# Rotary embedding of the queries moved into the score product, in the two chosen-token layers of a fused transformer kernel

## What is computed

```python
scores = h @ w_router                       # one score for each of the 1024 tokens
idx = sort(top_k(scores, 128))              # 128 tokens are chosen
x = hidden[idx]; pos = idx
h = rms_norm(x, ln1_w)
q = (h @ wq + bq)                           # 16 heads of 128
k = (h @ wk + bk); v = (h @ wv + bv)        # 8 heads of 128
q = q * cos + rotate_half(q) * sin          # rotary embedding by the token's place
k = k * cos + rotate_half(k) * sin
att = softmax(mask(q @ k.T / sqrt(128)))    # 128 x 128 for each of the 16 heads
x1 = x + (att @ v) @ wo
mlp = silu(rms_norm(x1) @ w_gate) * (rms_norm(x1) @ w_up) @ w_down
out[idx] = gate * (x1 + mlp) + (1 - gate) * x
```

## Time and profile before

| | |
|---|---|
| median of 3 runs | 1484.77 us (1483.41 to 1485.47) |
| profiled execution | 1484.15 us, of which the profile's span covers 1482.9 us |
| TensorE busy | 1408.4 us (95%) |
| VectorE busy | 1074.2 us (72%) |
| ScalarE busy | 1044.8 us (70%) |
| GpSimd busy | 686.9 us (46%) |
| mean granted TensorE clock | 0.982 of full speed |

### The profile page before, as it was taken

One profiled execution on the slowest core, in us unless ns is written; L12 is line 12 of the kernel. 1 busy time (PEld: TensorE's weight loads), 2 busy tenths in 40 slices (PEclk: granted clock), 3 DMA queues, 4 the chain that ended last, 5 costly groups with the idle time before them and its releaser, 6 DMA issues.

```text
span 1482.9 us, 23456 instructions
## 1 busy us (share of the span) xinstructions
PE 1408.4 (95%) x8326; PEld 1207.0 (81%) x8326; DVE 1074.2 (72%) x2453; ACT 1044.8 (70%) x2284; POOL 686.9 (46%) x830
## 2 busy tenths in 40 slices
PE   7899999999999998998999999999999978979899
PEld 6789898888888886787888888888897876657677
DVE  6989898989898985667766757766666737567634
ACT  4898989999898987575655655655654755585754
POOL 6576777676776646142333333433321130823223
PEclk9999999999999999999999999999999998998999
DMA  2000000000000000610000000000003332000000
GB/s 75 2 19 1 19 9 12 1 19 19 1 8 2 15 1 1 270 37 22 16 21 8 30 22 8 26 25 15 1 8 140 132 119 82 0 1 1 0 0 29
DMA packets 14340, 45.12 MB, mean 30 GB/s; under 512 B 3216, under 2 KB 3216, under 8 KB 12048
## 3 DMA queue, kind: packets, MB, share of 16 engines
q1 hardware_dynamic: 14224, 43.61, 8.2%
HBM read 42.55 MB, written 1.05 MB: 29 GB/s over the span
## 4 chain that ended last, share of the span: by engine, by line
PE 73%; DVE 16%; ACT 7%; issue 2%; POOL 1%; DVEq 0%; ACTq 0%; POOLq 0%
PE ps L149 32%; PE ps L355 16%; PE ps L344 10%; PE ps L1189 6%; DVE a_pT_lo L411 3%; DVE a_prob L364 2%; PE ps L2057 2%; PE ps L2063 2%; DVE a_q L694 1%; PE ps L2073 1%; PE ps L2076 1%; PE ps L614 1%; PE ps L2059 1%; PE ps L1964 1%; DVE h L2326 1%
## 5 line engine op out<-in xcount | busy, mean ns | idle before, releaser
L386 POOL TENSOR_SCALAR a_prob<-a_prob,a_rowinv 128x128 f32<-128x128 f32 (+7 forms) x256 | 188.4, 751 | 132.6 <-DVE a_rowinv L380 132.4
L411 DVE TENSOR_TENSOR a_pT_lo<-ps,a_pT_hi 128x512 fp32r<-128x512 f32 (+3 forms) x384 | 194.7, 550 | 21.0 <-ACT a_pT_hi L403 19.3
L364 DVE CUSTOM_DVE_ANT_0 a_prob<-ps,a_mask 128x128 f32<-128x128 f32 (+7 forms) x256 | 187.0, 749 | 21.1 <-PE ps L149 20.9
L371 ACT ACTIVATE a_prob<-a_prob,a_negmax 128x128 f32<-128x128 f32 (+7 forms) x256 | 197.3, 778 | 2.2 <-DVE a_negmax L364 1.5
L386 POOL TENSOR_SCALAR b_prob<-b_prob,b_rowinv 128x128 f32<-128x128 f32 (+7 forms) x128 | 94.4, 749 | 199.5 <-DVE b_rowinv L380 199.4
L403 ACT ACTIVATE a_pT_hi<-ps 128x512 fp32r<-128x512 f32 (+3 forms) x384 | 167.3, 492 | 24.7 <-PE ps L344 15.5
L344 PE MATMUL ps<-ident,a_prob 128*128 128x128 f32 x1152 | 160.2, 275 | 7.0 <-DVE a_pT_lo L411 5.5
L371 ACT ACTIVATE b_prob<-b_prob,b_negmax 128x128 f32<-128x128 f32 (+7 forms) x128 | 99.6, 779 | 72.5 <-DVE b_negmax L364 71.7
L344 PEld LDWEIGHTS ps<-ident,a_prob 128*128 128x128 f32 x1152 | 130.0, 140 | 20.5 <-POOL a_prob L386 7.9
L149 PE MATMUL ps<-a_k_hi,a_q 128*128 128x512 f32 (+3 forms) x384 | 140.3, 373 | 1.8 <-DVE a_negmax L364 1.2
L355 PE MATMUL ps<-a_pT_hi,a_v 128*128 128x512 f32 (+3 forms) x384 | 131.2, 349 | 1.1 <-DVE a_pT_lo L411 0.6
(11 more groups left out here) (479 smaller groups left out, 4005.7 us busy)
## 6 DMA issues: line engine op xcount, KB each, us to landing
f_wq<-in_f_wq SPq DMA_DIRECT2D x2, 2048.0 KB, 8.9
f_wo<-in_f_wo SPq DMA_DIRECT2D x2, 2048.0 KB, 18.0
b_w_raw<-in_b_qk SPq DMA_DIRECT2D x16, 256.0 KB, 2.6
a_w_raw<-in_a_w SPq DMA_DIRECT2D x8, 384.0 KB, 3.2
a_vo<-in_a_o SPq DMA_DIRECT2D x8, 256.0 KB, 2.6
f_wk<-in_f_wk SPq DMA_DIRECT2D x2, 1024.0 KB, 11.0
f_wv<-in_f_wv SPq DMA_DIRECT2D x2, 1024.0 KB, 13.0
f_wg<-in_f_wg SPq DMA_DIRECT2D x2, 1024.0 KB, 19.9
```

Source lines behind the costliest of these rows:

```text
L364: dve.tensor_tensor_reduce(slot(a, u), g.ps_flat[:, bank * HALF:bank * HALF + width], a.mask[:, N - width:], -1.0, -MASKED, ALU.add, ALU.m ...
L371: act.activation(prob, prob, ACT.Exp, bias=a.negmax[:, n:n + 1], scale=-1.0, accum_out=a.rowsum[:, n:n + 1]).then_inc(*g.exped.mark(a.tag, u))
L386: pool.tensor_scalar(prob, prob, a.rowinv[:, n:n + 1], 1.0, ALU.mult, ALU.mult).then_inc(*g.normed.mark(a.tag, u))
L411: dve.tensor_tensor(lo, src, fr(hi), ALU.subtract).then_inc(*g.lo.mark(a.tag, u, j0 // 4))
```

## The change

The queries are no longer rotated before the score product. Since the exchange of halves is a permutation of features, the product of rotated keys and rotated queries is written as two products into the same place: the rotated keys with queries times cosine, and the exchanged copy of the rotated keys with queries times the signed sine of the other half. The keys are made first (`F_ORDER`), the key blocks are rotated as before, and ScalarE makes an exchanged copy of each rotated key block (`k_turned`). All four `scores` come ahead of `values` on TensorE, and the four groups of exponentials ahead of the copies of values on ScalarE. `f.prob` holds the queries times sine until the exponentials overwrite it.

```diff
-F_ORDER = (4, 0, 1, 5, 2, 3)
+F_ORDER = (4, 5, 0, 1, 2, 3)
-F_SWAPPED = (1, 3, 5)
+F_SWAPPED = (1,)
@@ ffn_pe
     def scores(n):
-        pe.wait_ge(*dve.at(tag, "qk", (1, 2, 4, 5)[n]))
+        pe.wait_ge(*dve.at(tag, "turned", n + 2))
+        pe.wait_ge(*act.at(tag, "k_turned", n // 2))
         for j in range(4):
-            hd, out = 4 * n + j, bank[4 + n][:, j * P:j * P + P]
-            mm(out, f.qk[:, hd], f.qk[:, F_HEADS + hd * F_KV // F_HEADS], True, False)
+            hd, kv, out = 4 * n + j, (4 * n + j) * F_KV // F_HEADS, bank[4 + n][:, j * P:j * P + P]
+            mm(out, f.qk[:, hd], f.qk[:, F_HEADS + kv], True, False)
+            mm(out, f.prob[:, hd], f.swap[:, kv // 4, kv % 4], False, False)
             t = mm(out, f.ident_b[:], f.mask[:], False, True)
@@ ffn_pe, order
     scores(0)
+    scores(1)
+    scores(2)
+    scores(3)
     values(0)
-    scores(1)
     values(1)
-    scores(2)
     turn_prob(0)
-    scores(3)
     turn_prob(1)
@@ ffn_act, after the eviction of block p
-                t = act.activation(f.swap[dst, p % 2], f.qkb[src, p % 2], ACT.Copy)
+                t = act.activation(f.r2[dst, p % 2], f.qkb[src, p % 2], ACT.Copy)
+        if p in (2, 3):
+            c = p - 2
+            act.wait_ge(*dve.at(tag, "qk", c))
+            for src, dst in ((ROWS[1], ROWS[0]), (ROWS[0], ROWS[1])):
+                t = act.activation(f.swap[dst, c], f.qk[src, F_HEADS + 4 * c:F_HEADS + 4 * c + 4], ACT.Copy)
+            t.then_inc(*done.mark(tag, "k_turned", c))
@@ ffn_act, order
-    scores(0); values(0); scores(1); values(1); scores(2); turned(0); scores(3); turned(1)
+    scores(0); scores(1); scores(2); scores(3); values(0); turned(0); values(1); turned(1)
@@ ffn_dve, turn(p)
         dve.tensor_tensor(out, f.qkb[:, par], cos, ALU.mult)
+        if F_ORDER[p] < 4:
+            part = f.prob[:, 4 * F_ORDER[p]:4 * F_ORDER[p] + 4]
+            t = dve.tensor_tensor(part, f.qkb[:, par], f.ropes[:, 2].unsqueeze(1).broadcast_to([P, 4, P]), ALU.mult)
+            t.then_inc(*done.mark(tag, "turned", p))
+            return
@@ ffn_dve, order
     turn(3)
+    turn(4)
     most(0)
-    turn(4)
+    turn(5)
     most(1)
-    turn(5)
     divide(0)
```

More of the change, by code:

```diff
@@ L1499, in ffn_act @@
             for src, dst in ((ROWS[1], ROWS[0]), (ROWS[0], ROWS[1])):
-                t = act.activation(f.swap[dst, p % 2], f.qkb[src, p % 2], ACT.Copy)
+                t = act.activation(f.r2[dst, p % 2], f.qkb[src, p % 2], ACT.Copy)
             t.then_inc(*done.mark(tag, "swap", p))
+        if p in (2, 3):
[4 more added lines that the diff above has]
+            t.then_inc(*done.mark(tag, "k_turned", c))
     scores(0)
+    scores(1)
+    scores(2)
+    scores(3)
     values(0)
-    scores(1)
+    turned(0)
     values(1)
-    scores(2)
-    turned(0)
-    scores(3)
     turned(1)
@@ L1633, in turn @@
         dve.tensor_tensor(out, f.qkb[:, par], cos, ALU.mult)
+        if F_ORDER[p] < 4:
[3 more added lines that the diff above has]
+            return
         if p in F_SWAPPED:
             dve.wait_ge(*act.at(tag, "swap", p))
-            t = dve.tensor_tensor(f.r2[:, par], f.swap[:, par], sin, ALU.mult)
+            t = dve.tensor_tensor(f.r2[:, par], f.r2[:, par], sin, ALU.mult)
         else:
```

## The result

| | before | changed | ratio, 95% interval |
|---|---|---|---|
| first comparison, 10 runs each | 1485.05 us | 1487.82 us | 1.002 (1.001 to 1.0029) |
| second comparison, 19 and 8 runs | 1483.92 us | 1488.54 us | 1.0027 (1.0016 to 1.0037) |
| profiled execution (its span) | 1484.15 (1482.9) | 1489.33 (1488.0) | |

The change makes the kernel slower. The medians differ by 2.8 us in the first comparison and by 4.6 us in the second; from the ratios and their intervals it is 3.0 us (1.5 to 4.3) and 4.0 us (2.4 to 5.5). Forecast was + 4.8 us (1489.6, range 1486.9 to 1492.6).

The account below looks back on a forecast made before the run. The prediction took TensorE's full stream as the bound: + 3.57 us of products less waits of 0.50 and 0.62, taken as + 2.4 a stage, + 4.8 for two. That gave 1484.77 + 4.8 = 1489.6 us, range 1486.9 to 1492.6.

Parts of the forecast that it names:

- TensorE's list bounds, VectorE's chain runs beside it: Chosen-token layers: TensorE's full stream sets the end; at most 1.64 us a stage could be won from its waits.
- The 3.89 us in which PEld was free: Evidence against the forecast: weight loads free for 3.89 of 23.87 us, more than the new products' 3.57 us.
- The price of the products: TensorE's scores: 16 more float32 products a stage at 0.223 us each, + 3.57 us.
- The waits: TensorE's three waits: those of 0.50 and 0.62 us go, 0.52 ahead of `weigh(0)` stays; stage sum + 2.45.
- ScalarE's new places cost nothing: ScalarE's moved exchanges and evictions: same work, query blocks at least 1.5 us early for TensorE, so no cost.
- The spare 1.5 us: Smallest margin between VectorE's finished query blocks and TensorE's need of them, if each `scores` takes 2.17 us.
- The order costs nothing: Everything else on TensorE's list is the same and only reordered, charged at zero.
- no gain by itself: VectorE's 4.14 us less work a stage is covered by TensorE's full stream and gains nothing by itself.
- The rival on the clock: Last products of the two layers: shifted timing moves the granted clock's fall, 1.4 us either way; chance 16%.
- rival 4: Clock fall enters the first layer (1491.0 us) or leaves the second (1488.2); chance 16%, half each way.
- rival 2: All three of TensorE's waits in the stretch go: + 3.9 us, 1488.6 us; chance 9%.
- rival 4's better half: The shift takes the clock's fall out of the second layer: - 1.4 us, 1488.2; half of the 16% chance.

Follow-up runs that it names:

- e1: Kernel before with each of the 16 score products issued twice in each layer, VectorE and ScalarE untouched: 1489.75 us, ratio 1.0037.
- e2: Changed kernel with the second product of each score (exchanged keys times queries' sine part) left out: 1483.39 us, ratio 0.9998.
- e5: Kernel before with each score product issued four times, 48 more products a layer: 1505.61 us, ratio 1.0138.
- e7: Kernel before with only the change's order, queries rotated as before and one product a score: 1489.79 us, ratio 1.0036.
- e3: Kernel before with only a new order: third and fourth scores and first transposes ahead of router product, third maximum before first division: 1481.53 us, ratio 0.9982.
- e8: The changed kernel again, unaltered, in 8 runs beside 19 of the kernel before: 1488.54 us, ratio 1.0027.

## Why the prediction was right, point by point

**TensorE's list bounds, VectorE's chain runs beside it.** Shown. e1 costs 3.02 us a layer with VectorE untouched, and e2 gains 0.17 us with VectorE over a quarter lighter. The chain of waits of before named VectorE alone for 16 us; what told the truth was TensorE's row without a hole next to it. The 3.89 us in which PEld was free were no room either, and the trace of before says why. Before the scores, in a stream of 128-column products, PEld was busy for 7.99 of 8 us; 1.9 us of its free time lie in the two groups of values with their 512 columns (busy 0.81 of 1.77 and 0.82 of 1.78 us), in which PE was never idle, and most of the rest in the three waits.

**The price of the products.** Right for one product: 0.223 us was forecast, and 0.223 is the growth of a head in place (a score head starts 0.556 us after the one before, where it was 0.333) and 0.224 by e5. But the four groups take 8.84 us where they took 4 x 1.28 = 5.12, + 3.72 and not + 3.57. The 0.15 us are no rounding. A group's first head takes 0.28 us when it follows other work and 0.33 when it follows a mask (633.73, 634.01 and 634.34 before). In the old order all four groups open with the short slot, in the new one only the first: three times 0.055.

**The waits.** Two of three go, and the one ahead of `weigh(0)` stays with 0.34 us idle, the row forecast. Sum forecast + 2.45, taken as + 2.4; measured + 2.40 and + 2.39. That it fits to a hundredth is in part luck. From start to start the parts are + 3.72 for the score groups, - 0.55 for the transposes up to `weigh(0)`, - 0.62 for the wait ahead of `weigh(1)`, - 0.10 for `weigh(1)` itself, and - 0.06 for the values, which now stand in one row. The 0.15 us of the score groups, which the prediction didn't have, are made up by the values and by slots behind waits that shrank more than the 0.05 it allowed.

**ScalarE's new places cost nothing.** Right, for a reason that the prediction gave only in part. TensorE met no wait because the new products keep it busy while ScalarE works: with them gone (e2), TensorE stands 0.2 and 0.4 us idle for the last two query blocks. The spare 1.5 us that it counted were made by the load that it charged.

**The order costs nothing.** The prediction charged the reordering of TensorE's list at zero ("the same and only reordered"). In the changed kernel TensorE has no pause from it. By itself the order costs 2.15 us in f1 (e7), and with 16 products VectorE's shorter list is worth 2.32 us in it. The prediction put both at nothing, and they nearly cancel: that the sum came out is luck in this part, since neither was reckoned. VectorE's saving was not worthless, as "no gain by itself" says; it was needed to undo what the change's own order did.

**The rival on the clock.** TensorE's last products of f1 and f2 in the changed kernel, to be held against the earlier trace rows:

```profile
678.96 1.19 PE L1189 MATMUL ps<-f_takeT,f_step_hi 128*128 128x512 f32 x2 [3.44 <-ACT f_step_hi L1549]
...
683.68 0.63 PE L1189 MATMUL ps<-f_takeT,f_chT_lo 128*128 128x512 f32 x2
...
1220.28 0.70 PE L1189 MATMUL ps<-f_takeT,f_step_hi 128*128 128x512 f32 x2 [3.44 <-ACT f_step_hi L1549]
...
1225.17 0.63 PE L1189 MATMUL ps<-f_takeT,f_chT_lo 128*128 128x512 f32 x2
```

```profile
678.00:682.00 4.00, 3.04 (x7) 2.48 (x8) 2.08 (x4) 1.01 (x2) 0.00 (x0) 0.57 0.02 4
```

In f1 they took 3.30 us before and take 4.72 now (granted clock 0.57 over the 4 us shown, which begin in the pause), and f2 has kept its own fall (4.89 against 4.68). That is the outcome that rival 4 described. That the shift caused it is not shown: in e2 and e3 these products of f1 start at 675.50 and 675.40 us, within 0.2 us of before's 675.30, and take 5.92 and 4.63 us. Over all nine profiled executions they take 3.28 to 6.05 us in either layer, and only before's f1 and e7's f2 escaped, so the 1.4 us of the prediction is too small for this term. Outside the two stretches the profiled executions differ by + 1.25 us ahead of f1, which the change doesn't touch, + 0.73 between the layers, and - 1.67 after f2, where the work is the same to the instruction:

```profile
661.25:1177.19 515.94, 508.94 (x3090) 445.94 (x3088) 347.38 (x781) 296.88 (x658) 171.01 (x227) 0.99 0.11 37
1203.45:1488.00 284.55, 244.51 (x1092) 188.91 (x1090) 167.17 (x268) 169.90 (x239) 91.13 (x65) 0.93 0.08 30
```

Before, the same two parts took 515.21 and 286.22 us. So the profiled executions stand 5.1 us apart, of which 4.8 are the change's. Over the nine profiled executions the span less the two stretches runs from 1432.6 (e2) to 1436.5 us (e5), with 1435.2 for before and 1435.5 and 1434.3 for the two of the changed kernel: these show nothing that is given back elsewhere, within a spread of 3.9 us that is not the change's.

**The size of the whole.** The forecast of + 4.8 us lies outside the first comparison's interval (1.5 to 4.3 us) and inside the second's (2.4 to 5.5). The mechanism was right, and its size right where it acts. Both medians (1487.82 and 1488.54 us) lie near the prices of rival 2 (1488.6) and of rival 4's better half (1488.2). Rival 2 is excluded by its own condition, since one wait is left. Of rival 4's better half the two traces show this much: neither f1 nor f2 lost its fall, but behind f2 the changed kernel takes 284.5 us both times (1203.45 to 1488.0, and 1202.28 to 1486.8 in e8), 1.7 less than before with the same work. What the total keeps is 3.5 us at like clock; about 1.3 us less than the stretches add up to is left open. e5 excludes that the same share (a quarter) is given back, but its interval of 3 us each way cannot exclude a fixed 1.3. The term that this corrects is the clock's: the prediction took 1.4 us for it, the runs of one unchanged kernel spread over 6.7 us, and a kernel's median moves with them.

## What to carry to other kernels

When the chain of waits names one engine, look at the other engines in the same stretch before its work is taken away: an engine next to it without a hole is as much a bound, and moving work onto it costs nearly its full price at once. Work that stands between two dependent groups is cover; an order that gathers the dependent groups loses it, and a change that brings both a new order and a saving should be taken apart, since one may only pay for the other. Where an engine's own waits add up to 1.6 us, ask first which independent work in its list could stand there: the plain reorder (0.70 us a layer) gained more than the new arithmetic could have with its products for nothing (0.17).

## What the runs showed of the hardware that was not expected

In e7 the granted clock fell from 1.00 to 0.50 for about 6 us in f2, during the last of three pauses of 0.32, 1.18 and 1.10 us between score groups, and it did not fall in f1 with the same pauses (29.14 and 26.02 us). An unchanged kernel spread over 1480.1 to 1486.4 us on one chip and 1479.7 to 1486.3 on another, with a mean granted clock between 0.985 and 0.978, while its two stretches, without a fall, both took 23.87 us. A float32 product of 128 columns took 0.22 us to the next start when it followed another float32 product, and 0.28 when it followed a bfloat16 mask (before, 633.73 to 633.95 and 634.01 to 634.29), so the mask costs the stream more than its own slot.
